# First layer norm of a decoder kernel: deviations in batches of 2, 2 and 4 tiles, normalising moved from ScalarE to VectorE, warm-up matmuls on TensorE

## The reference, cut to what matters

```python
def _layernorm(x, axis=-1, eps=1e-05):
    m = jnp.mean(x, axis=axis, keepdims=True)
    v = jnp.var(x, axis=axis, keepdims=True)
    return (x - m) / jnp.sqrt(v + eps)

x = x + _L0_attn_ref(_layernorm(x), w_q, w_k, w_v, w_o)      # 32 heads of 128, 8 kv groups
x = x + _L0_xattn_ref(ctx_4096, ctx_4096, _layernorm(x))
x = x + _L0_ffn_ref(_layernorm(x), gate..., up..., down...)  # 4-bit weights
```

## Time and profile before

| what | us |
|---|---|
| median of 3 runs (856.58 to 858.5) | 857.33 |
| span of the profiled execution | 852.7 |
| median less that span | 4.6 |
| PE busy | 802.8 (94%) |
| DVE / ACT / POOL busy | 446.4 / 364.2 / 329.1 |
| first projection matmul starts | 18.82 |
| first scores of group 0 start | 40.52 |

### The profile page before, as it was taken

The page is one execution under the profiler, slowest core; times in us unless marked ns, Lnnn a source line. Parts: engine busy times, 40 slices in busy tenths (PEclk is TensorE's granted clock), DMA queues, the critical chain, the costliest instruction groups (busy, mean ns, idle before and its releaser), DMA issues.

```text
span 852.7 us, 11954 instructions
## 1 busy us (share of the span) xinstructions
PE 802.8 (94%) x3944; PEld 666.1 (78%) x3944; DVE 446.4 (52%) x731; ACT 364.2 (43%) x969; POOL 329.1 (39%) x400
## 2 busy tenths in 40 slices
PE   3999999999999999999999999999889988789898
PEld 2788888888888888888888888888767766667686
DVE  3235425524434443443344355366887877677672
ACT  4355435526435553552554455266644222212112
POOL 6443223214223331331432242135575474746550
PEclk9999999999999999999999999999999989999999
DMA  8610002002000200200200020001001222221322
GB/s 265 210 51 1 26 0 98 12 12 98 0 25 2 96 20 5 98 0 25 72 26 25 0 98 0 0 1 42 2 13 44 65 50 67 47 47 41 81 76 99
DMA packets 60822, 41.33 MB, mean 48 GB/s; under 512 B 28348, under 2 KB 48156, under 8 KB 60796
## 3 DMA queue, kind: packets, MB, share of 16 engines
q1 hardware_dynamic: 60796, 41.01, 16.3%
HBM read 38.90 MB, written 2.10 MB: 48 GB/s over the span
## 4 chain that ended last, share of the span: by engine, by line
PE 73%; DVE 11%; issue 5%; POOL 5%; SPq 2%; ACT 2%; DMA 2%; POOLq 0%; DVEq 0%; ACTq 0%
PE psum L345 21%; PE psum L347 20%; PE psum L346 20%; PE psum L466 6%; PE psum L475 3%; DMA f_z<-in_L_ffn_up_zeros 2%; SPq L281 2%; POOL f_w L890 1%; DVE f_m L1141 1%; DVE f_zn L1135 1%; DVE negmax L1067 1%; PE psum L351 1%; PE psum L365 1%; DVE rowmax L1065 1%; DVE probs L1061 1%
## 5 line engine op out<-in xcount | busy, mean ns | idle before, releaser
L865 POOL TENSOR_TENSOR probs<-probs,rowinv 128x512 f32<-128x512 f32 x64 | 66.8, 1043 | 321.9 <-DVE rowinv L1080 321.9
L695 ACT ACTIVATE probs<-probs,negmax 128x128 f32<-128x128 f32 x256 | 99.8, 391 | 79.1 <-DVE negmax L1067 79.1
L345 PE MATMUL psum<-xt_hi,wq_hi 128*128 128x512 f32 x256 | 104.5, 408 | 0.0
L1061 DVE TENSOR_TENSOR probs<-psum,causal 128x512 f32<-128x512 f32 x64 | 44.2, 690 | 109.5 <-PE psum L466 109.5
L345 PE MATMUL psum<-wo_hi,at_hi 128*128 128x512 f32 x256 | 100.4, 392 | 0.5 <-DVE at_lo L1098 0.5
L347 PE MATMUL psum<-xt_hi,wq_lo 128*128 128x512 f32 x256 | 100.3, 392 | 0.0
L346 PE MATMUL psum<-xt_lo,wq_hi 128*128 128x512 f32 x256 | 100.0, 390 | 0.0
L347 PE MATMUL psum<-wo_hi,at_lo 128*128 128x512 f32 x256 | 99.9, 390 | 0.0
L346 PE MATMUL psum<-wo_lo,at_hi 128*128 128x512 f32 x256 | 99.8, 390 | 0.0
L345 PE MATMUL psum<-ft_hi,f_hi 128*128 128x512 f32 (+1 forms) x176 | 72.3, 411 | 20.5 <-POOL f_lo L895 18.1
L688 ACT CAST pt_hi<-psum 128x512 fp32r<-128x512 f32 x64 | 37.6, 587 | 121.9 <-PE psum L475 121.9
(11 more groups left out here) (117 smaller groups left out, 1717.6 us busy)
## 6 DMA issues: line engine op xcount, KB each, us to landing
wq_raw<-in_L_attn_w_q SPq DMA_DIRECT2D x8, 1024.0 KB, 5.6
wo_raw<-in_L_attn_w_o SPq DMA_DIRECT2D x8, 1024.0 KB, 7.8
f_q<-in_L_ffn_gate_qweight SPq DMA_DIRECT2D x40, 64.0 KB, 2.3
f_q<-in_L_ffn_up_qweight SPq DMA_DIRECT2D x40, 64.0 KB, 3.5
f_q<-in_L_ffn_down_qweight SPq DMA_DIRECT2D x10, 256.0 KB, 3.2
xacc<-in_x SPq DMA_DIRECT2D x8, 256.0 KB, 5.6
wk_raw<-in_L_attn_w_k SPq DMA_DIRECT2D x8, 256.0 KB, 2.6
wv_raw<-in_L_attn_w_v SPq DMA_DIRECT2D x8, 256.0 KB, 2.7
```

The costliest lines, as they stand in the source:

```text
L345: pe.matmul(dst, a_hi, b_hi, start=start, stop=False)
L695: e = act.activation(probs[:, t % 2, j, :], probs[:, t % 2, j, :], ACT.Exp, bias=negmax[:, t % 2, j:j + 1], scale=SCALE, accum_out=rowsum[ ...
L865: pool.tensor_tensor(probs[:, t % 2], probs[:, t % 2], rowinv[:, t % 2, :].unsqueeze(2).to_broadcast([P, HG, P]), ALU.mult).then_inc(prob_ ...
L1061: dve.tensor_tensor(probs[:, r], psum[:, BK_S, :].rearrange("p (a b) -> p a b", a=HG), causal[:].unsqueeze(1).to_broadcast([P, HG, P]), AL ...
```

## The change

It has four parts.

- **POOL, `inverse_deviations`:** the deviations of the first norm come in three chains, tiles 0 and 1, tiles 2 and 3, tiles 4 to 7. A chain waits until the last of its tiles is counted, and has six steps on 2 or 4 columns; the step for `shift` is gone. The splits of k and v stand between the second and the third chain, those of q0 to q3 behind the third.
- **DVE, `first_norm`:** normalising is a `tensor_scalar` on DVE (x less mean, times deviation). DVE counts tiles 0 to 3, then normalises them with the lo parts in between, and only behind the lo part of tile 3 counts tiles 4 to 7 and goes on to their normalising.
- **ACT:** it has no `normalise` in the first norm; it copies tile i, rounds a weight block, and from tile 5 on copies out a projection.
- **PE, `warm`:** 14 matmuls of `ident` by `ident` (128 columns, float32) as soon as the constants are there, and 3 more behind each of the first four turns. They write PSUM bank 0, which nothing reads before the first scores write it anew.

```diff
+    DEVIATIONS = [(0, 2), (2, 2), (4, 4)]
+    BATCH = [0, 0, 1, 1, 2, 2, 2, 2]
+    WARM_FIRST, WARM_NEXT = 14, 3
...
+            def warm(n):
+
+                for _ in range(n):
+                    pe.matmul(psum[:, BK_S, 0:P], ident[:], ident[:], start=True, stop=True)
+
             pe.wait_ge(consts_pool, 4)
+            warm(WARM_FIRST)
             for b in range(NB):
...
                 turn_tile((BK_T, BK_VT)[b % 2], xn[:, b % 2, :]).then_inc(ln_turned[0], 1)
+                if b < BH:
+                    warm(WARM_NEXT)
...
-            for i in range(NB + 1):
-                if i < NB:
-                    normalise(i, 0, xn)
-                if i >= 1:
-                    tile_first(i - 1, 0, xt_hi, (BK_T, BK_VT)[(i - 1) % 2])
-                if 1 <= i <= FIRST_UNITS:
-                    first_unit(i - 1)
-                if i >= BH + 2:
-                    j = i - BH - 2
+            for i in range(NB):
+                tile_first(i, 0, xt_hi, (BK_T, BK_VT)[i % 2])
+                if i < FIRST_UNITS:
+                    first_unit(i)
+                if i >= BH + 1:
+                    j = i - BH - 1
...
+            def inverse_deviations(i):
+
+                b, n = DEVIATIONS[i]
+                v, r, w = vareps[:, b:b + n], rstd[:, b:b + n], newton[:, b:b + n]
+                pool.wait_ge(var_ready[0], b + n)
+                after(pool.tensor_scalar(v, meanvar[:, b:b + n, 1], EPS, 1.0, ALU.add, ALU.mult))
+                after(pool.tensor_tensor(r, v, halfneg[:].to_broadcast([P, n]), ALU.pow))
+                after(pool.tensor_tensor(w, r, r, ALU.mult))
+                after(pool.tensor_tensor(w, w, v, ALU.mult))
+                after(pool.tensor_scalar(w, w, -0.5, 1.5, ALU.mult, ALU.add))
+                pool.tensor_tensor(r, r, w, ALU.mult).then_inc(rstd_ready[0], 1)
...
-            for b in range(NB):
-                inverse_deviation(b, 0)
-                if b >= BH:
-                    split_second(HBLK[b - BH], b - BH + 1)
-            for i in range(NB - BH, FIRST_UNITS):
+            inverse_deviations(0)
+            inverse_deviations(1)
+            split_second(HBLK[0], 1)
+            split_second(HBLK[1], 2)
+            inverse_deviations(2)
+            for i in range(2, FIRST_UNITS):
                 split_second(HBLK[i], i + 1)
...
-            for i in range(NB + 2):
-                if i < NB:
-                    dve.wait_ge(ld_x[i], 16)
-                    count(i, 0)
-                if i >= 2:
-                    tile_second(i - 2, 0, xt_hi, xt_lo, (BK_T, BK_VT)[i % 2])
+            def first_norm(b):
+
+                dve.wait_ge(rstd_ready[0], BATCH[b] + 1)
+                if b >= 2:
+                    dve.wait_ge(ln_turned[0], b - 1)
+                dve.tensor_scalar(xn[:, b % 2, :], xacc[:, b, :], meanvar[:, b, 0:1], rstd[:, b:b + 1],
+                                  ALU.subtract, ALU.mult).then_inc(ln_ready[0], 1)
...
+            for b in range(BH):
+                first_count(b)
+            for b in range(BH):
+                first_norm(b)
+                if b >= 1:
+                    first_second(b - 1)
+            first_second(BH - 1)
+            for b in range(BH, NB):
+                first_count(b)
+            for b in range(BH, NB):
+                first_norm(b)
+                if b > BH:
+                    first_second(b - 1)
+            first_second(NB - 1)
```

More of the change, by code:

```diff
@@ L978, in tile_second, with first_count, first_second @@
                                   hi[:, :, cols].bitcast(F32), ALU.subtract).then_inc(ln_lo[k], 1)
-            for i in range(NB + 2):
-                if i < NB:
-                    dve.wait_ge(ld_x[i], 16)
-                    count(i, 0)
-                if i >= 2:
-                    tile_second(i - 2, 0, xt_hi, xt_lo, (BK_T, BK_VT)[i % 2])
+            def first_norm(b):
[4 more added lines that the diff above has]
+                                  ALU.subtract, ALU.mult).then_inc(ln_ready[0], 1)
+            def first_count(b):
+                dve.wait_ge(ld_x[b], 16)
+                count(b, 0)
+            def first_second(b):
+                tile_second(b, 0, xt_hi, xt_lo, (BK_T, BK_VT)[b % 2])
+            for b in range(BH):
[12 more added lines that the diff above has]
+            first_second(NB - 1)
             dve.wait_ge(consts_pool, 7)
```

## The result

| kernel | median of 20 runs, us | lowest to highest |
|---|---|---|
| before | 856.12 | 852.65 to 858.5 |
| changed | 860.03 | 856.71 to 862.7 |

The ratio is 1.0044 with a 95% interval of 1.0029 to 1.0058: slower by 0.44%, some 3.8 us (2.5 to 5.0). Where a gain or a loss of the whole time is given in us, it is the ratio less one, times the median of before. In each execution the whole time is 1.8 to 2.0 us above the span of that same execution. So of the 4.6 us that were taken as lying outside the span, some 2.7 only say that the profiled execution of before was a quick one. The forecast adds a difference to the median, and this doesn't touch it.

The account below looks back on a forecast made before the run. TensorE, busy 802.8 of 852.7 us, was taken to bound the kernel, so the start of its dense work counts. Start +3.6 and clock -0.4 gave +3.2 us, 857.33 becoming 860.5; the 8-in-10 range was 858.0 to 862.5.

Parts of the forecast that it names:

- lo part of tile 3 ends: First half of the tiles: VectorE finishes tile 3's lo part at 14.75 us instead of 18.76, bounds 13.4 to 15.8.
- four counts: VectorE counts tiles 4 to 7 only after tile 3's lo part, taking 3.5 us, to 18.3.
- power step on 2 and on 4 columns: POOL's deviation chains: the power step costs 0.2 us more on two columns and 0.55 more on four.
- chain with its pick-up: POOL's chain over tiles 4 to 7 takes 0.15 + 1.93 + 0.55 us, ending at 20.9.
- tile 4 normalised, handed over: VectorE normalises tile 4 behind POOL's last chain, 0.55 us with its handover.
- turn until the next matmul: TensorE's four transposes of tile 4 at the low clock take 0.85 us until the next matmul can start.
- first k matmul: The first projection on TensorE starts at 22.4 us against 18.82, 3.6 us later.
- low stretch of the clock: TensorE's first projection again starts at the low clock, which lasts 4.4 us, the mean of three stretches.
- start to first scores against before: Clock term behind the first k matmul: -0.4 us for a shorter low clock, with ends of -1.2 and +0.5.
- worse: Head: power step pays per column, tile 4's normalising loses to the q0 split, low clock lasts; +5.1, 862.4; chance 0.11.
- the kept clock: Rival: TensorE's clock stays high over the idle time before tile 4's turn; +0.8 us, 858.1; chance 0.04.
- Absorbed later: Rival: the front's delay is taken up where TensorE waits for others, 18.1 us for POOL's `f_lo`; 858; chance 0.04.

Follow-up runs that it names:

- e7: Changed kernel with the counts of e6 and the first four projections each ahead of a second-half turn: first k 17.61, first scores 40.07, ratio 0.9996 to before.
- f1: Changed kernel reordered: k, v, q0 splits behind normalisings, k, v, q0 projections ahead of tile 4's turn, 6 last warm-ups: first k 14.09, ratio 0.9920 to before.
- e3: Changed kernel with 38 warm-up matmuls instead of 3 behind the turn of tile 3: first k 22.67, first scores 41.88, ratio 1.0021 to before.
- e4: Changed kernel with POOL waiting before the q0 split until tile 4 is normalised: first k 22.18, first scores 42.91, ratio 1.0032 to before.
- e6: Changed kernel with counts of tiles 4 to 7 taken out of their block and x loaded ahead of q: first k 21.56, ratio 1.0038 to before.
- e1: Kernel before with the warm-up matmuls alone, 14 ahead and 3 behind each of the first four turns: first scores 39.07, ratio 0.9996 to before.
- e2: Changed kernel without any warm-up matmuls: first k 24.17, first scores 45.14, ratio 1.0061 to before.

## Why the prediction was right

It said 860.5 and slower; the runs say 860.03. The terms, against the rows of after (those up to the first k matmul add up to 22.3; the 22.4 comes of rounding on the way):

| step of the sum | predicted | measured |
|---|---|---|
| lo part of tile 3 ends | 14.75 | 15.12 |
| four counts | 3.5 | 3.2 |
| power step on 2 and on 4 columns | 0.76, 1.1 | 0.73, 1.01 |
| chain with its pick-up | 2.63 | 2.50 |
| tile 4 normalised, handed over | 0.55 | 1.55 |
| turn until the next matmul | 0.85 | 0.77 |
| first k matmul | 22.4 | 23.13 |
| low stretch of the clock | 4.4 | 4.8 |
| start to first scores against before | -0.4 | -0.35 |
| sum | +3.2 | +3.96 in the head, +3.8 in the runs |

The place was right: the wait that ends last had moved from the lo part of tile 3 to the turn of tile 4, and from the first scores to the turn near 595 us nothing was gained or lost. e7 and f1 show it from the other side, since with the projection ahead of that turn the start follows the lo part again. The low clock was right too: e3 priced it at 2.6 us where I had 2.4 and a quicker turn.

Two terms were mis-sized, and both by the same fact. I let tile 4's normalising start first and put its collision with the q0 split into the rival "worse"; it is 1.0 us and on the path (e4 takes 0.95 of it back), which covers the miss of 0.76 in the head. In the first half I had the normalising of tiles 0 and 1 cost POOL's second chain 0.5 to 1.0 us and tile 2 go undisturbed. It was the other way: the second chain ran 7.67 to 9.84, 0.06 longer than the first, and tile 2 lost 1.0 us to the k split. That the two errors in the first half nearly cancelled, 14.75 against 15.12, is luck and no merit of the sum. Another 0.2 of the late start is in the landing of the first tile (3.59 for 3.39).

The -0.4 for the clock met -0.35, and that is in part luck too. From the first k matmul on, the low clock lasted 3.4 us in e4 and 5.3 in e7. At 0.475 us for each microsecond that is a spread of 0.9 us; with the 3.4 of e4 the head would have lost some 3.3 us (an estimate from these rows). The end of +0.5 that the prediction gave this term has no row behind it: the longest stretch in its rows, 5.3 us, gives 0. It also had the q splits done by 26; the last ended at 31.2, and no matmul waited for it.

The Trainium skill ("SBUF — State Buffer", Who interferes with whom) says that of the two, whoever issues first has the shared ports for its whole instruction and the other is blocked. The rows agree: a normalising takes 0.54 us alone and 1.50 where the split began first, and it ends 0.3 us behind the end of the split (11.65 against 11.36).

Of the rivals, the kept clock did not occur in the change, but e3 made it occur and gave 41.88. "Absorbed later" is dead: in the changed kernel and all ten experiments the distance to before at the turn near 595 us is within 0.1 us of that at the first scores, from -6.8 to +4.6. The whole times of the runs follow within 1.4 us.

Where I was wrong was in the experiments: e6 and e7 fell short because I took a count in a gap to be free without adding up the gaps, and e1 in part because a faster TensorE found ScalarE's copy late. And the bounds that I had drawn for the clock, high after 1.98 us of idle time and low after 3.16, are too simple: it was low after 2.25 us in e7, and fell without any idle time above 1.1 us in e1, where TensorE was half busy. What exactly lets it fall stays open.

## What to carry to other kernels

Before a chain is batched, look at what stands behind the last of its batches in the order of the busiest engine: here the change won 3.6 us on the path that the profile named (to the lo part of tile 3) and lost 8 on the one that came next (from there to the first k matmul). Warm-up matmuls are worth what the stretch behind them lets them keep; put the last ones right ahead of the work, and look whether the engines behind can follow. Where VectorE and POOL meet on the path, a wait that lets the critical one go first cost nothing here and started the first projection 2.2 us earlier.

## What the hardware showed that I had not expected

- A near tie decides a microsecond: POOL's split began 0.05 us (tile 2) and 0.08 us (tile 4) ahead of the normalising, and each time the normalising took some 1.5 us instead of 0.54. Small operations get by with less: POOL's second chain lost 0.06 us to two normalisings in the changed kernel, and 0.36 in e6, where its first step fell into one.
- POOL's power step takes 0.56, 0.73 and 1.01 us on 1, 2 and 4 columns: about 0.15 per further column, under half of what one column seemed to cost over a plain step.
- In e1 the granted clock fell to 0.59 and 0.56 in two stretches of 2 us, after TensorE had been busy for 0.95 and 1.17 of 2 us; it was busy for 1.78 and 1.46 in them, and the clock was back at 1.00 in the next.
- In the kernel before, the clock column reads 1.00 from 18 to 24 us though its matmuls stand 0.43 apart; e2, without warm-ups too, reads 1.00 at the same spacing. In after, with warm-ups, the column does show the low clock (0.50 from 18 us on). At the head of these traces the spacing of matmuls is to be trusted, not the column.
